# Expert scatters of a transformer layer: from paced groups to one run, with slots cleared six rows at a time

## What is computed

```
logits = xt @ Wg.T
topk_logits, topk_idx = jax.lax.top_k(logits, TOP_K)
w = jax.nn.softmax(topk_logits, axis=-1)
gates = jnp.zeros((T, N_EXPERTS), xt.dtype).at[rows, topk_idx].add(w)
...
y = jnp.einsum('te,teh->th', gates, o)
```

## Time and profile before

| what | value |
|---|---|
| median of 3 runs | 753.11 us (751.09 to 756.80) |
| the profiled execution | 753.37 us |
| its span, first to last instruction | 751.3 us |
| mean granted TensorE clock | 0.877 |
| PE, DVE, ACT, POOL busy | 674.6, 529.0, 442.2, 267.6 us |
| chain that ended last | PE 67%, DVE 17%, ACT 7%, issue 5% |

### The profile page before, as it was taken

One profiled execution on the slowest core, in us unless ns is written; L12 is line 12 of the kernel. 1 busy time (PEld: TensorE's weight loads), 2 busy tenths in 40 slices (PEclk: granted clock), 3 DMA queues, 4 the chain that ended last, 5 costly groups with the idle time before them and its releaser, 6 DMA issues.

```text
span 751.3 us, 14474 instructions
## 1 busy us (share of the span) xinstructions
PE 674.6 (90%) x4866; PEld 392.8 (52%) x4866; DVE 529.0 (70%) x1797; ACT 442.2 (59%) x656; POOL 267.6 (36%) x431
## 2 busy tenths in 40 slices
PE   6899777989888999989999999988999999999987
PEld 5674333434334655555665555645565555556533
DVE  6758886568575666767667687778668676777676
ACT  4223453445436666757667675767577776677654
POOL 5813146455560423322332323222333233232411
PEclk9555795587758979999999999999899999999989
DMA  6651963033334743626053443535252615340075
GB/s 160 194 113 19 237 170 111 32 88 103 119 83 116 200 149 77 189 59 197 24 126 105 113 125 96 165 82 176 60 137 69 188 44 138 124 117 12 26 185 156
DMA packets 99289, 87.93 MB, mean 117 GB/s; under 512 B 13296, under 2 KB 86704, under 8 KB 99216
## 3 DMA queue, kind: packets, MB, share of 16 engines
q1 hardware_dynamic: 94320, 76.69, 38.1%
q0 software_dynamic: 4544, 9.35, 3.7%
q10 hardware_dynamic: 352, 0.97, 0.6%
HBM read 49.79 MB, written 20.80 MB: 94 GB/s over the span
## 4 chain that ended last, share of the span: by engine, by line
PE 67%; DVE 17%; ACT 7%; issue 5%; another core or an unknown queue 2%; DMA 1%; POOL 0%; ACTq 0%; DVEq 0%
PE ov L923 18%; PE aux L886 15%; PE aux L984 10%; DVE junk L1123 7%; ACT probs L791 3%; PE aux L936 3%; PE sc L906 3%; PE sc L840 3%; PE aux L941 3%; DVE maxes L1121 2%; PE sc L841 2%; PE sc L842 2%; PE aux L964 1%; PE aux L957 1%
## 5 line engine op out<-in xcount | busy, mean ns | idle before, releaser
L791 ACT ACTIVATE probs<-sc 128x1024 f32<-128x1024 f32 (+1 forms) x320 | 287.2, 941 | 194.1 <-PE sc L906 165.4
L1123 DVE CUSTOM_DVE_ANT_0 junk<-aux,cst 128x128 bf16<-128x128 f32 (+3 forms) x512 | 220.3, 486 | 34.6 <-PE aux L886 30.6
L886 PE MATMUL aux<-kT,qT 32*128 32x512 f32 (+3 forms) x768 | 207.0, 461 | 41.0 <-DVE maxes L1123 9.3
L1121 DVE TENSOR_REDUCE maxes<-aux 128x1 f32<-128x512 f32 x256 | 163.3, 683 | 46.0 <-PE aux L886 37.9
L707 POOL TENSOR_SCALAR_AFFINE_SELECT probs<-probs 128x256 f32<-128x256 f32 x224 | 88.4, 408 | 286.5 <-ACT probs L791 281.7
L923 PE MATMUL ov<-probs,v 128*32 128x512 f32 (+3 forms) x1536 | 178.4, 555 | 0.6 <-POOL probs L707 0.5
L886 PEld LDWEIGHTS aux<-kT,qT 32*128 32x128 f32 x768 | 94.0, 205 | 132.2 <-issue 32.9
L906 PE MATMUL sc<-qT,kT 32*128 32x512 f32 (+3 forms) x768 | 146.1, 438 | 5.8 <-DMA qT<-mT 3.3
L722 POOL DMA_INDIRECT ys<-ysb,back x78 | 75.5, 969 | 103.6 <-DVE ysb L1171 58.8
L984 PEld LDWEIGHTS aux<-w2all,hid 128*128 128x128 f32 x624 | 78.5, 198 | 39.2 <-DVE maxes L1121 22.6
L984 PE MATMUL aux<-w2all,hid 128*128 128x128 f32 x624 | 90.6, 290 | 0.3 <-DVE kql L1060 0.3
(11 more groups left out here) (121 smaller groups left out, 604.0 us busy)
## 6 DMA issues: line engine op xcount, KB each, us to landing
w1b<-w_scr SPq DMA_DIRECT2D x39, 512.0 KB, 4.8
w2all<-in_L_ffn_W SPq DMA_DIRECT2D x39, 256.0 KB, 3.2
xs<-ysb SPq DMA_DIRECT2D x13, 387.0 KB, 8.2
kT<-kqh SPq DMA_DIRECT2D x32, 128.0 KB
w_scr<-w1b SPq DMA_DIRECT2D x8, 512.0 KB
qT<-kqh SPq DMA_DIRECT2D x30, 128.0 KB
xrow<-in_L_attn_x SPq DMA_DIRECT2D x7, 512.0 KB, 6.4
xsin<-xs SPq DMA_DIRECT2D x9, 387.0 KB
```

Of the source, the lines that this page charges most:

```text
L791: nc.scalar.activation(probs[:, s % 2, 2 * half:2 * half + 2, 0:cols], pair(part)[:, :, 0:cols], ACT.Exp).then_inc(sc_done, 1)
L886: last_ = nc.tensor.matmul(bank(part)[:, at:at + cols], qT[n % 3][rows, P * i:P * i + P], kT[n % 3][rows, k0:k0 + cols], start=True, stop= ...
L1121: last_ = nc.vector.reduce_max(dst, src, axis=AX.X)
L1123: last_ = nc.vector.tensor_tensor_reduce(out=junk[:, AUXI[part] % 3, at:at + cols], in0=src, in1=cmask[:, W - cols:W], scale=1.0, scalar=L ...
```

## The change

All 64 scatters stand in the list behind step 9 of unit 0, in the order of choice and tile. The wait for the steps' exponentials (`PACED`) is gone; the waits of the first scatter of each choice stay. The 13 clears still have 768 rows each, but a partition of `zrow` now fills six neighbouring rows of `xs` instead of six rows that lie 128 apart, and the constants for column 128 follow that. `SCHED` is otherwise the same.

```diff
--- before.py
+++ after.py
@@ -81,7 +81,6 @@
 PIECES = 13
 SCATTERS = (1, 2)
-SCATTER_FROM, SCATTER_STEPS = 8, 24
 VECTOR_NORMS = 3
@@ -265,9 +264,8 @@
-        step = NS * n + s - SCATTER_FROM
-        if 0 <= step < SCATTER_STEPS:
-            parts.extend([("scatter", 0, 0)] * (TOPK * NT * (step + 1) // SCATTER_STEPS - TOPK * NT * step // SCATTER_STEPS))
+        if (n, s) == (SCATTERS[0] - 1, NS - 1):
+            parts.extend(("scatter", t, k) for k in range(TOPK) for t in range(NT))
@@ -325,9 +323,7 @@
-    parts = fill(parts)
-    scatters = iter([(t, k) for k in range(TOPK) for t in range(NT)])
-    return [("scatter",) + next(scatters) if x[0] == "scatter" else x for x in parts]
+    return fill(parts)
@@ -358,10 +354,6 @@
-PACED = {x: [y for y in SCHED[:i] if y[0] == "scores"][-1] for i, x in enumerate(SCHED)
-         if x[0] == "scatter" and any(y[0] == "scores" for y in SCHED[:i])}
@@ -568,7 +560,7 @@
-                    sp.dma_start(xs.rearrange("(g v p) c -> g p v c", p=P, v=SPARE)[i], zrow).then_inc(xs_zero, 16)
+                    sp.dma_start(xs.rearrange("(g p v) c -> g p v c", p=P, v=SPARE)[i], zrow).then_inc(xs_zero, 16)
@@ -685,8 +677,6 @@
                 elif what == "scatter":
                     t, k = part[1:]
-                    if part in PACED:
-                        pool.wait_ge(sc_done, PAIRI[PACED[part]] + 1)
@@ -1204,7 +1194,7 @@
-    c[:, K_DEST + TOPK * NT:] = TOPK * TOK + P * np.arange(SPARE)[None, :] + np.arange(P)[:, None]
+    c[:, K_DEST + TOPK * NT:] = TOPK * TOK + np.arange(SPARE)[None, :] + SPARE * np.arange(P)[:, None]
```

## The result

The changed kernel takes 810.73 us (median of 4 runs, 808.45 to 811.64) against 752.20 us for the kernel before (4 runs): a ratio of 1.078, 95% interval 1.073 to 1.082. Forecast were 765 us and a range of 744 to 785 us. The direction was right; the loss is 58 us instead of 12. The profiled execution took 811.64 us, with a span of 809.9 us. A median in this document is that of all runs of a kernel; a ratio compares undisturbed runs alone, since some executions fall into a slower state, so that it can differ a little from the quotient of the medians.

The account below looks back on a forecast made before the run. PE (busy 90% of the span), or what it waits for, was taken to bound the kernel, with PE's updates told late during unbroken scatters. 753.4 + 11.9 (steps beside the run) + 0 (all else) = 765.3 us; range 744 to 785 us.

Parts of the forecast that it names:

- Where to look: The span grows in 114 to 240 us alone; unit 0 stays within 1 us.
- Start and length: Run of 64 scatters on POOL begins at 114.0 us, 1.26 us apart plus 2.8 us mid-run, ending at 197.6 us.
- Reading of the gaps: ACT's long gaps in 102 to 235 us: while POOL issues indirect DMAs without pause, others learn late what PE finished.
- The steps beside the run: Units 1 and 2: 12.9 steps at 6.46 us beside the run, 9.1 at 4.43 after; 123.9 against 112.0 us, +11.9 us.
- second rival: Beside the run: what is held stays held until a run ends, at the worst window's rate; +36.7 us, 790 us; chance 0.10.
- The clock: PE's granted clock stays near 0.5 to 0.6 beside the run; so the rate of long runs at lower clock was chosen.
- bound of 97.5 us: Lower bound for the 22 steps from 114.2 us, all at the calm 4.43 us a step: -14.5 us.
- third rival: Units 1 and 2: scatters never held PE, so the whole stretch goes at the calm rate; -14.5 us, 739 us; chance 0.12.
- Clears at 0: The 13 clears with longer packets change nothing, as nobody waits for them: 0, with 0.9 us to either side.
- POOL's cover: POOL's next duty, unit 3's first select, is reached only after the run is over, so queueing behind it costs 0.
- load of rows: SP's load of the first group's rows keeps its place in order; scatters landing 28 us earlier buy 0, at best 0.7 us.

Follow-up runs that it names:

- e6: Changed kernel with each scatter replaced by a 128 x 1024 memset on POOL and two plain DMAs bringing the rows: 731.53 us (kernel before 753.78 us).
- e8: Changed kernel with each scatter replaced by a plain POOL DMA of the same rows to consecutive slots: 738.02 us (kernel before 753.78 us).
- e7: Changed kernel with a 128 x 1024 memset on POOL ahead of each scatter, starts 2.13 us apart: 786.45 us (kernel before 753.78 us).
- e10: Changed kernel with a 128 x 512 memset on POOL ahead of each scatter: 754.78 us.
- e2: Changed kernel with the clears of the kernel before, on the chip where the latter takes 731.6 us: 727.71 us, ratio 0.997.
- e1: Kernel before with the clears of the changed kernel, scatters as before, on the chip where the kernel before takes 731.6 us: 733.44 us, ratio 1.003.
- r2: The same file as e2 (changed kernel with the old clears), run on another chip: 804.10 us, ratio 1.065 to the kernel before.
- r1: The changed kernel itself, run again beside the kernel before on another chip: 807.35 us, ratio 1.070.
- e3: Changed kernel with each scatter waiting for the landing of the one before, on the chip where the kernel before takes 731.6 us: 821.75 us, ratio 1.127.
- e13: e10 with DVE also clearing unit 3's triangles and SP's first load of rows also waiting for the memsets: 746.89 us, ratio 0.986 to the kernel before.
- e9: Changed kernel with a 128 x 64 memset on POOL ahead of each scatter: 800.12 us.
- e15: Changed kernel with a 128 x 256 memset on POOL ahead of each scatter: 767.85 us.

## Why the prediction was right or wrong

- **Where to look.** Right. Unit 0 is unchanged (20 exponentials from 50 to 110 us in both), the steps behind the run go at 4.3 us, and 54.9 of the 58 us are lost in units 1 and 2.
- **Start and length.** The run began at 111.5 instead of 114.0 us. I had moved the two scatters of step 8 out of the way, but left the last selects and the last subtraction of w1b where they stood behind them. Its length was 82.5 us for 83.6: 64 times 1.26 and a pause of 1.9 us. The 2.33 us that I took for the wait for the first 32 landings end, by the row, with ACT's exponential, so they were the pacing's; the wait for the landing is 1.36 us. Neither error changed the sum by more than 3 us.
- **Reading of the gaps.** Right: "while POOL issues indirect DMAs without a pause, what PE finishes is told to the others late". e6 and e8 take the indirect DMAs away and the gaps go; e7 and e10 keep all 64 and only set them apart, and the gaps go as well. One support of it was misread: the 78 result DMAs don't all go singly, some stand in pairs 1.3 us apart; it is long runs that the kernel before lacks there.
- **The steps beside the run: the step that failed.** I took "6.46 us, that of long runs at the lower clock", 12.9 steps in 83.6 us. It was 3 steps in 83 us, 28 us each, 6 exponentials for the forecast 26, and unit 3 began at 269.8 us instead of near 225. The 9.9 missing steps at 4.43 us are 44 us, and 765.3 + 44 = 809 us, which is the measured time to within 3 us. What was wrong was to take a rate from runs of five to ten scatters, as if each scatter of a long run cost what one of a short run does. The trace after shows that it doesn't: two steps start in the first 9 us, about the length of the longest runs before, and one in the 75 us behind. The second rival (held until a run ends, 790 us) went the right way, but its rate, the worst window's 11.5 us a step, was too mild by more than half, and the hold is not total: ACT goes on at 133.00, 147.03 and 191.16 us, all before the last scatter ends at 194.05.
- **The clock.** Right in the run (0.52 against "0.5 to 0.6"), but it doesn't set the price. e2 and e10 have the same scatters and 0.83 and 0.84 in the same stretch. In the changed kernel it is 0.50 from 120 to 200 us, in which PE is busy for 10.5 us of 80; half the speed can't make 28 us of a step of 4.4. Choosing among the rates by the clock hid what the price was.
- **The bound of 97.5 us for the stretch** ("at 4.43 us all through") is what a chip without hold gives, and the third rival's 739 us is 11 us above what I measured there: 727.7 us for the run, 731.6 us for the kernel before. The Trainium skill's page "SBUF — State Buffer", section "SBUF: two separate sides", says that PE and ACT never wait on anyone; it says so of the ports of SBUF. My third rival made of it that scatters can't cost PE anything, which is more than the page says. In the first measurement PE stood for 48.80 us beside a POOL that did nothing but send indirect DMAs, and taking these apart freed it (e10); no run shows that a port is what it waited for, so the rule itself is neither borne out nor refuted. No trace of the kernel before on one chip could have told that the third rival holds on another.
- **Clears at 0.** Right, by e1 (1.003, 1.000 to 1.007), by r2 against r1 where there is a hold (804.1 and 807.4 us), and by the DMA share that fell while the engines' busy time stayed.
- **POOL's cover, and the load of rows.** Both right for the changed kernel: POOL waited 76.9 us for its first select, and the load of the first rows went out at 282.18 us, 88 us behind the last scatter. Both stop being free as soon as the hold is gone: 94.4 us (e3) and 26.0 us (e10) for the one, 14.9 us (e13) for the other.
- **What stays open.** Why one chip holds nothing. All that is shown is that the kind goes with the session: none of the 25 runs of the kernel before in session 1 is above 735.4 us, and none in the other sessions or the first measurement is below 742.2. Whether it is the chip or something else that stays for a session can't be told apart. Then, what the updates wait for: the landing of a scatter isn't late in the run (the copy at 153.41 us waited 1.36 us for it, and 1.43 us in e2 on the chip without hold), so a queue of unfinished scatters is not seen. And whether it takes the indirect form or the scattered writes that come with it (e8 changed both).

## What to carry to other kernels

Read the distance between a queue's instructions, not only their sum: on the chips that hold, 64 indirect DMAs cost 76 us when they start 1.3 us apart and nothing at 1.7 us. When gaps grow with the length of a burst, a price taken from short bursts can be far too low for a long one; price the long one by "nothing moves while it lasts" as well (here that would have been 83 us of standstill, close to the 75.9 us that were lost in units 1 and 2 against e2). And before a stall is taken for a law of the hardware, or its absence for one, run the same file on a second chip.

## What the runs showed of the hardware

- A run of 64 indirect DMAs of POOL, 1.26 us from start to start (1.29 on average), all but stops PE, DVE and ACT in the first measurement and in session 2: three steps in 83 us, with 43.5 us in which ACT, and 48.8 us in which PE, start nothing (the changed kernel). Starts 1.37 us apart on average hold nearly as much (e9), 1.5 us a little under half (e15), 1.7 us nothing (e10).
- What comes late is what PE has finished (58 us in the longest case); what ACT has finished is taken up within 0.03 us in the same stretch.
- On the chip of session 1 the run shows none of it (41 exponentials in e2, 6 in r2, which is the same file on another chip).
- Plain DMAs of POOL with the same rows to consecutive slots, 0.54 us each, don't do it (e8, 738.02 us), nor do memsets (e6, 731.53 us).
- The kernel before loses some 20 us of its 752 to the same effect on the chips that hold: units 1 and 2 take 102.9 us there, and 81.3 us on the other (e1_clears_only, with the same paced scatters).
